# Two attention outputs and their values, copied and scaled in other places, in a hand-ordered pipeline

## The reference, cut to what matters

```
x = x + tanh(g0[0]) * attention_0(context, context, layernorm(x))   # A: 16 heads, softmax over the HEADS
x = x + tanh(g1[0]) * gated_mlp(layernorm(x))                       # B: silu(gate) * up, hidden width 768
x = x + tanh(g0[1]) * attention_1(layernorm(x), context)            # C: 16 query heads, one key and value head
x = x + tanh(g1[1]) * (layernorm(x) @ (W + low_rank).T + b)         # D
```

## Time and profile before

| | |
|---|---|
| median of 3 runs | 2359.47 us (2358.21 to 2359.94) |
| the profiled execution | 2358.72 us, of which the traced span is 2356.9 us |
| busy in the span | PE 98%, DVE 93%, POOL 75%, ACT 72% |
| granted TensorE clock | 0.999 of full speed over the span |
| start, loop of 57 iterations, end | about 165, 2009 and 183 us of the span |

### The profile page before, as it was taken

The page is one execution under the profiler, slowest core; times in us unless marked ns, Lnnn a source line. Parts: engine busy times, 40 slices in busy tenths (PEclk is TensorE's granted clock), DMA queues, the critical chain, the costliest instruction groups (busy, mean ns, idle before and its releaser), DMA issues.

```text
span 2356.9 us, 69621 instructions
## 1 busy us (share of the span) xinstructions
PE 2308.5 (98%) x27827; PEld 2062.3 (87%) x27827; DVE 2200.9 (93%) x3613; ACT 1705.6 (72%) x3402; POOL 1777.8 (75%) x2512
## 2 busy tenths in 40 slices
PE   6999999999999999999999999999999999999998
PEld 5888888889888888888889889889889889889887
DVE  6999999999999999999999999999999999999973
ACT  4667777777777777777777777777777777777664
POOL 3767787787787787787787777777778778778754
PEclk9999999999999999999999999999999999999999
DMA  3000010010010010010010100100100100000000
GB/s 110 28 22 28 29 34 27 29 34 27 29 34 27 29 34 27 29 34 27 31 33 27 34 29 27 34 29 27 34 29 28 33 29 30 31 29 32 20 22 15
DMA packets 74332, 73.33 MB, mean 31 GB/s; under 512 B 6555, under 2 KB 73393, under 8 KB 74290
## 3 DMA queue, kind: packets, MB, share of 16 engines
q1 hardware_dynamic: 74290, 72.75, 9.9%
HBM read 54.90 MB, written 16.78 MB: 30 GB/s over the span
## 4 chain that ended last, share of the span: by engine, by line
PE 56%; DVE 37%; issue 3%; ACT 1%; POOL 1%; DMA 1%; SPq 0%; POOLq 0%; DVEq 0%; ACTq 0%
DVE m L1600 11%; PE work L2383 10%; PE work L2384 9%; PE work L2385 9%; PE scores L2480 6%; PE work L2513 5%; PE work L2500 5%; DVE scores L1597 5%; DVE m L1591 4%; PE work L2420 4%; PE scores L2470 4%; DVE x L1628 4%; PE work L2398 2%; DVE stats_B L1559 2%; DVE stats_D L1559 2%
## 5 line engine op out<-in xcount | busy, mean ns | idle before, releaser
L856 ACT ACTIVATE e<-scores 120x1024 f32<-120x1024 f32 x512 | 517.5, 1042 | 35.9 <-DVE scores L1597 21.5
L2383 PE MATMUL work<-xt_hi_B,w_hi 128*128 128x256 f32 x1536 | 445.0, 290 | 2.8 <-POOL xt_lo_B L426 2.8
L2384 PE MATMUL work<-xt_lo_B,w_hi 128*128 128x256 f32 x1536 | 426.9, 278 | 0.0
L2385 PE MATMUL work<-xt_hi_B,w_lo 128*128 128x256 f32 x1536 | 426.6, 278 | 0.0
L413 POOL TENSOR_TENSOR zt<-e 120x512 f32<-120x512 f32 x256 | 331.1, 1295 | 49.5 <-ACT e L856 40.9
L407 POOL TENSOR_TENSOR h_lo<-h_f,h_hi 128x256 fp32r<-128x256 f32 x384 | 278.9, 740 | 90.5 <-ACT h_hi L803 90.4
L1597 DVE TENSOR_TENSOR scores<-scores,m 120x1024 f32<-120x1024 f32 x256 | 303.0, 1227 | 4.2
L2383 PEld LDWEIGHTS work<-xt_hi_B,w_hi 128*128 128x128 f32 x1536 | 290.8, 189 | 17.0 <-POOL xt_lo_B L426 13.5
L1609 DVE TENSOR_TENSOR e<-e,work 120x2048 f32<-120x2048 f32 x128 | 291.4, 2276 | 0.2
L1591 DVE TENSOR_REDUCE m<-scores 120x128 fp32r<-120x2048 f32 x128 | 290.0, 2266 | 0.9 <-PE scores L2470 0.8
L2384 PEld LDWEIGHTS work<-xt_lo_B,w_hi 128*128 128x128 f32 x1536 | 289.3, 188 | 0.0
(11 more groups left out here) (224 smaller groups left out, 7290.6 us busy)
## 6 DMA issues: line engine op xcount, KB each, us to landing
x_ln<-xp SPq DMA_DIRECT2D x64, 256.0 KB, 2.9
x_res<-xp SPq DMA_DIRECT2D x64, 256.0 KB, 2.8
y<-y_out SPq DMA_DIRECT2D x64, 256.0 KB, 2.2
ctx_f_A<-cp SPq DMA_DIRECT2D x64, 128.0 KB, 2.1
ctx_f_C<-cp SPq DMA_DIRECT2D x64, 128.0 KB, 2.0
qm<-mT SPq DMA_DIRECT2D x256, 4.0 KB
e<-wi SPq DMA_DIRECT2D x3, 768.0 KB, 7.1
w_ctx<-wc SPq DMA_DIRECT2D x1, 656.0 KB
```

Of the source, the lines that this page charges most:

```text
L856: return act.activation(e[0:SC, c, 2 * h:2 * h + 2, :, :].rearrange("p a b n -> p (a b n)"), scores[0:SC, 2 * h:2 * h + 2, :].rearrange("p ...
L2383: pe.matmul(out, a_hi, b_hi_, start=first, stop=False, skip_group_check=parts)
L2384: pe.matmul(out, a_hi, b_lo_, start=False, stop=False, skip_group_check=parts)
L2385: last = pe.matmul(out, a_lo, b_hi_, start=False, stop=end, skip_group_check=parts)
```

## The change

- `attended0`'s result is copied out of PSUM whole by ScalarE (`attended_out`, into `y0f`, which lies where the raw key weights of A lay in `w_ctx`); `y_hi["A"]` is then rounded from that copy, and `y_lo["A"]` is made by GpSimd (`attended_lo`), no longer by VectorE.
- C's values are made with A's: the two weights lie side by side in `w_ctx`, and `values0` has 272 columns in place of 256. `keys_values1` becomes `keys1`. Since A runs several rows ahead of C, the 16 columns pass through a ring of three small tiles (`v1_ring`), moved on by ScalarE once in each iteration, before they land in `v1_one`. `w_ctx` is loaded by four DMAs in place of one.
- The reciprocals of C's sums are written to PSUM (`W[1]`), and `weigh` reads them there; `rz_q` is gone.
- The order of all five streams is new, with other banks; the loop is cut at another place (it begins before `gate_up(4)`, no longer before D's product) and has 56 iterations.

```diff
-DEPTH = 7
+DEPTH = 8
-CSEG = {"k0": 0, "v0": KC * D, "k1": 2 * KC * D, "v1": 2 * KC * D + KC * P}
+CSEG = {"k0": 0, "v0": KC * D, "k1": KC * D + KC * (D + HD)}
+        v1_ring = sb("v1_ring", [P, 3, HD])
-        rz_q = sb("rz_q", [P, KC, 2, S // 32])
+        y0f = w_ctx[:, CSEG["k0"]:CSEG["k0"] + KC * D].rearrange("p (k n) -> p k n", k=KC)
...
-            sp.dma_start(w_ctx[:, :], wc).then_inc(s["ld_cst"], 16)
+            both_values = w_ctx[:, CSEG["v0"]:CSEG["k1"]].rearrange("p (k n) -> p k n", k=KC)
+            sp.dma_start(w_ctx[:, 0:KC * D], wc[:, FROM["k0"]:FROM["v0"]]).then_inc(s["ld_cst"], 16)
...
+            def attended_lo():
+                return pool.tensor_tensor(y_lo["A"][:, :, :], y0f[:, :, :], y_hi["A"][:, :, :].bitcast(F32), ALU.subtract)
...
+            def attended_out(bank):
+                return act.activation(y0f[:, :, :], two(bank, KC), ACT.Copy)
...
             def values1_out(bank):
-                return act.activation(v1_one[0:SC, 0:HD], bank[0:SC, P:P + HD], ACT.Copy)
+                return act.activation(v1_ring[0:SC, 0, :], bank[0:SC, D:D + HD], ACT.Copy)
+            def values1_on(i):
+                to = v1_ring[0:SC, i + 1, :] if i < 2 else v1_one[0:SC, 0:HD]
+                return act.activation(to, v1_ring[0:SC, i, :], ACT.Copy)
...
-            def reciprocal1():
-                return dve.reciprocal(rz_q[:, :, :, :], yz_q[:, :, :, :, HD])
+            def query_sums(bank):
+                return bank[:, 0:KC * 2 * (S // 32)].rearrange("p (c h q) -> p c h q", c=KC, h=2)
+            def reciprocal1(bank):
+                return dve.reciprocal(query_sums(bank), yz_q[:, :, :, :, HD])
...
             def values0(bank):
-                    last = pe.matmul(bank[:, 0:D], ctx_f["A"][:, kc, :], wc_of("v0", kc * D, D),
+                    last = pe.matmul(bank[:, 0:D + HD], ctx_f["A"][:, kc, :], wc_of("v0", kc * (D + HD), D + HD),
...
-                for kc in range(KC):
-                    last = pe.matmul(bank[:, P:P + HD], ctx_f["C"][:, kc, :], wc_of("v1", kc * HD, HD),
```

More of the change, by code:

```diff
@@ L1983, in _ @@
                 mean_variance("D").then_inc(s["ln_eps_D"], 1)
-                low(y_lo["A"][:, :, :], two(W[1], KC), y_hi["A"][:, :, :]).then_inc(s["yA_lo"], 1)
                 dve.wait_ge(s["M1_mm"], t)
@@ L2341, in _ @@
+            key_max(0).then_inc(s["M0_max"], 1)
             dve.wait_ge(s["woC_mm"], LAST + 6)
@@ new lines, in _ @@
+            pe.wait_ge(s["yz1"], 9)
+            gate_up(W[1], 5).then_inc(s["G_mm5"], 1)
+            pe.wait_ge(s["y_weighed"], 9)
+            pe.wait_ge(s["T_lo_C"], 9)
+            queries(W[3], "C", "q1").then_inc(s["q_mm_C"], 1)
+            pe.wait_ge(s["yA_out"], 9)
+            down(W[2], 0)
+            down(W[2], 1)
+            pe.wait_ge(s["yC_lo"], 9)
+            pe.wait_ge(s["ends_act"], 66)
+            rows_out(W[0], y_hi["C"], y_lo["C"], "wo1").then_inc(s["woC_mm"], 1)
+            down(W[2], 2)
@@ new lines, in _ @@
+            down(W[2], 3)
+            pe.wait_ge(s["A0_exp"], 20)
+            key_scores(1).then_inc(s["M1_mm"], 1)
+            down(W[2], 4)
+            pe.wait_ge(s["G_lo5"], 9)
+            down(W[2], 5).then_inc(s["dn_mm5"], 1)
+            rows_out(W[1], y_hi["A"], y_lo["A"], "wo0").then_inc(s["woA_mm"], 1)
+            values0(W[0]).then_inc(s["v0_mm"], 1)
+            pe.wait_ge(s["M1_max"], 9)
+            key_scores(0).then_inc(s["M0_mm"], 1)
+            pe.wait_ge(s["ln_D"], 9)
+            transposes(W[3], "D").then_inc(s["T_mm_D"], 1)
@@ new lines, in _ @@
+            pe.wait_ge(s["yA_out"], LAST + 3)
+            pe.wait_ge(s["ld_ctx_C"], 16 * (LAST + 3))
+            keys1(W[0]).then_inc(s["kv1_mm"], 1)
+            pe.wait_ge(s["yC_lo"], LAST + 3)
+            rows_out(W[3], y_hi["C"], y_lo["C"], "wo1").then_inc(s["woC_mm"], 1)
+            pe.wait_ge(s["ends_act"], 7 * LAST + 23)
+            down(W[2], 0)
+            down(W[2], 1)
+            down(W[2], 2)
+            down(W[2], 3)
+            pe.wait_ge(s["A0_exp"], 2 * LAST + 8)
+            key_scores(1).then_inc(s["M1_mm"], 1)
@@ new lines, in _ @@
+            down(W[2], 4)
+            pe.wait_ge(s["G_lo5"], LAST + 3)
+            down(W[2], 5).then_inc(s["dn_mm5"], 1)
+            pe.wait_ge(s["res_C"], LAST + 3)
+            rows_out(W[3], y_hi["A"], y_lo["A"], "wo0").then_inc(s["woA_mm"], 1)
+            pe.wait_ge(s["M1_max"], LAST + 3)
+            key_scores(0).then_inc(s["M0_mm"], 1)
+            pe.wait_ge(s["ln_D"], LAST + 3)
+            transposes(W[1], "D").then_inc(s["T_mm_D"], 1)
+            pe.wait_ge(s["res_B"], LAST + 3)
@@ new lines, in _ @@
+            pe.wait_ge(s["ld_ctx_C"], 16 * (LAST + 4))
+            keys1(W[0]).then_inc(s["kv1_mm"], 1)
+            pe.wait_ge(s["y_weighed"], LAST + 4)
+            down(W[2], 0)
+            down(W[2], 1)
+            pe.wait_ge(s["G_h4"], LAST + 4)
+            pe.wait_ge(s["T_lo_C"], LAST + 4)
+            queries(W[3], "C", "q1").then_inc(s["q_mm_C"], 1)
+            pe.wait_ge(s["ends_act"], 7 * LAST + 29)
+            pe.wait_ge(s["yC_lo"], LAST + 4)
+            rows_out(W[0], y_hi["C"], y_lo["C"], "wo1").then_inc(s["woC_mm"], 1)
@@ L3075, in _ @@
[L3075 to L3084 removed]
+            pe.wait_ge(s["ln_D"], LAST + 6)
```

3309 lines of the change are left out of this document (1803 added, 1506 removed), and 10 rows, old and new, of the table given.

## The result

The changed kernel takes 2332.23 us (median of 4 runs, 2331.37 to 2333.18), the kernel before in the same sessions 2358.84 us. The ratio is 0.9888, 95% interval 0.9874 to 0.9902: 1.1% faster, 0.8 us from the predicted 2333.0. The sum was nearly exact, but not every reason for it: the experiments show a third condition that the prediction did not have, and several of its smaller terms were wrong. So part of this closeness is luck.

What follows compares the result with a forecast made beforehand. VectorE and TensorE were taken to bound the loop in turn. -0.50 + 0.10 = -0.40 us per iteration, times 57 = -22.8, and -2.9 for the ends take the span from 2356.9 to 2331.2: 2333.0 us as an execution, range 2317 to 2348.

Steps and rivals of the forecast that it cites:

- VectorE's half, -0.50: From `yz_q` to `scores0(1)`: moving `y_lo["A"]` to GpSimd saves 0.50 us per iteration, limited by `key_scores(1)`.
- TensorE's account, -0.30: TensorE, per iteration: C's value matmuls save 0.37 us, wider `values0` costs 0.07; VectorE still releases `scores0(1)` last by 0.1.
- the rival in which TensorE becomes the bound: Loop: the iteration is what TensorE needs, 34.62 us, in all 2321 us; chance 0.15.
- `T_lo_B` late by 0.10: TensorE's half: `x_biased` ahead of `xt_lo_B` on GpSimd makes `T_lo_B` late, +0.10 us per iteration.
- Its upper bound: `T_lo_B`'s delay on GpSimd: at most 0.67 us per iteration, if only the last gap holds; half the gain gone.
- the range of this case: Whole kernel, the prediction's own case, chance 0.58: 2323 to 2344 us, from the bounds of `T_lo_B` and the ends.
- ScalarE's chain, nothing: ScalarE's new copy and moved keys cost nothing; `y_lo["C"]` is ready about 0.1 us before TensorE wants it.
- Reciprocals in PSUM, nothing: VectorE's reciprocals of C's sums, written to and read from PSUM, cost no more than in SBUF.
- A fixed price of 65 ns for PSUM: Rival on VectorE's half: reciprocal and two `y_q` cost 65 ns more each, +11 us, 2344 us; chance 0.05.
- The collision with `attended_lo`: Rival on VectorE's half: GpSimd's `attended_lo` holds up `y_q`, +0.54 us per iteration, 2364 us; chance 0.05.
- The ends, -2.9: Start and end: -2.1 us from TensorE's savings, +1.5 for SyncE's DMA issues, -2.3 for fewer fillers; together -2.9.
- the prediction's own signs of being wrong: Profile signs listed beforehand, among them a start over 165.5 us by more than 2, or its granted clock under 0.98.

Runs made afterwards that it cites:

- run 3: Kernel before, C's value matmuls and VectorE's `y_lo["A"]` both left out of the loop: ratio 0.9970, iteration 35.18 us.
- run 4: Kernel before with both those removals, and GpSimd's sum `y_out + x_biased` moved ahead of `y_lo["C"]`: ratio 0.9885, iteration mean 34.80 us.
- run 7: Changed kernel with four more matmuls on TensorE ahead of the wait for `M0_max`: ratio 0.9966 to the kernel before, iteration 35.22 us.
- run 6: Kernel before with four more matmuls on TensorE ahead of the wait for `M0_max` in the loop: ratio 1.0056, iteration 35.55 us.
- run 8: Changed kernel with the reciprocals of C's sums back in SBUF: ratio 0.9988 to the kernel before, iteration mean 35.22 us.
- run 11: Changed kernel with the four loads of `w_ctx` issued behind the fourth round of weights: ratio 0.9898 to the kernel before.
- run 12: Changed kernel with 22 filling matmuls in a gap of TensorE's start: ratio 0.9906 to the kernel before.
- run 9: Changed kernel with `y_lo["A"]` back on VectorE, from the copy in SBUF: ratio 0.9990 to the kernel before, iteration mean 35.30 us.

## Why the prediction was right, and where it was not

*VectorE's half, -0.50:* right in size and place: 0.48 measured, limited by `key_scores(1)` as it said, with 0.21 us of wait where its own sum left 0.08. But that VectorE's and TensorE's halves are all there is was wrong for the kernel before, as runs 3 and 4 show.

*TensorE's account, -0.30:* it was 0.39 or 0.40, since C's keys with values took 0.91 us start to start and the keys alone take 0.46 (1018.36 to 1018.82), with `values0` at 1.02 for 0.96. That VectorE still releases `scores0(1)` last, by about 0.1, holds: 0.06 by run 7. The wait before it was taken at 0.31 from the weight load's row; run 6 gives 0.13. The two errors offset each other (0.13 + 0.39 - 0.48 = 0.04 us left, by its own figures 0.31 + 0.30 - 0.50 = 0.11). So the rival in which TensorE becomes the bound was nearer in kind than its 2321 us, and its price too high: what it could have saved beyond the forecast was the wait that is left, 0.06 x 56 = 3.4 us, not 0.2 us per iteration.

*`T_lo_B` late by 0.10:* wrong. `xt_lo_B` starts 1037.21 - 1033.90 = 3.31 us behind `scores0(1)`, before 3.30, each time right behind ScalarE's `xt_hi_B`. That half did lose 0.08 us, elsewhere: `scores1(0)` now stands behind the second gate product, not the third, and from the first gate product of the row to the second `scores1` group it takes 8.84 us in place of 8.77, start to start, with one change of operand more. That this change is the cause is read from the trace and not tried. The term of 0.10 stands for nothing that happened, and the 0.08 that was lost elsewhere fits it by luck. Its upper bound was also misread: with 0.67 not half of the gain is gone but all of it, 0.67 - 0.50 = 0.17 us per iteration slower. And the range of this case does not add up: 11 and 3 us above 2333 are 2347, not 2344.

*ScalarE's chain, nothing:* right. `y_lo["C"]` ends 0.21 us ahead of its first product; there is no wait for it in the loop.

```profile
1021.60 1.30 POOL L624 TENSOR_TENSOR y_lo_C<-y1f,y_hi_C 128x512 fp32r<-128x512 f32 x1 [0.69 <-ACT y_hi_C L883]
```

*Reciprocals in PSUM, nothing:* right as a price. The first argument for it was empty, though: a line laid through 957 ns for 128 numbers and 354 ns for 32 leaves the same rest at both, whatever PSUM costs. What shows the price is the run. By form, after:

```profile
L1864 DVE TENSOR_TENSOR y_q<-yz_q,work 128x256 f32<-128x256 f32 x128 | 48.1, 417 | 2.1
L1860 DVE RECIPROCAL work<-yz_q 128x32 f32<-128x32 f32 x64 | 23.2, 362 | 2.1
```

417 ns and 362 ns stand against 419 and 354 before. The two rivals built on it are out. A fixed price of 65 ns for PSUM, which the table in "VectorE: DVE Perf Modes" of the Trainium skill, section on the TRN2 errata, would give (an estimate from its 120 and 58 cycles at 0.96 GHz), does not show: -2 and +8 ns. The collision with `attended_lo` comes only where both inputs lie in SBUF (run 8), and there it costs 0.39 us per iteration over 34.83 and not the rival's 0.54, since `key_max(1)` waits anyway.

*The ends, -2.9:* -3.7 by the traces (-26.5 in all, less 22.8), from parts of which at least two were wrong. The issues of SyncE cost nothing by the trace: TensorE's product from the last weights starts at 22.25 us, before at 22.65 (run 11 could not show it, for it delayed `w_ctx`). And the start, with 25 fillers fewer, is no shorter. There one of the prediction's own signs of being wrong came true: the granted clock over the start is 0.95, under its 0.98, and by `xt_lo_D` the start is more than 2 us longer. In the changed kernel TensorE is busy for 2.3 of the 8 us from 44 to 52 us, and its granted clock falls to 0.50, which is 1.2 GHz, from 48 to 60 us; in the kernel before it is busy for 7.4 of these 8 and the clock stays at 1.00. Windows of 2 us, the number behind DVE, ACT and POOL is PEclk:

```profile
46.00:48.00 2.00, 0.75 (x28) 0.56 (x21) 1.18 (x1) 1.37 (x5) 1.92 (x5) 0.79 0.00 0
48.00:50.00 2.00, 0.63 (x3) 0.63 (x4) 1.97 (x2) 1.32 (x3) 1.92 (x3) 0.50 0.00 0
...
58.00:60.00 2.00, 2.00 (x35) 1.76 (x32) 2.00 (x1) 0.00 (x0) 1.09 (x4) 0.50 0.00 0
```

A's queries there take 3 us at 0.21 us a matmul, and 1.5 in run 12, where the clock was back at 1.00. How much of the longer start is the clock's stays open, since run 12's fillers cost more than they gave. The start ended 2.2 us later, the drain of the last seven rows 5.6 us sooner: its distances of `xt_lo_D` sum to 208.4 us, before 213.9. Seven rows at the loop's 0.40 would be 2.8 of these; the rest I did not take apart. That the ends came within 1 us of the forecast is luck.

*What the prediction lacked* is the step from "two chains alternate" to "nothing else is near". It took the slack of TensorE and ScalarE to a tenth and never wrote down GpSimd's. With the old order the same removals give 0.05 us per iteration (run 3), with the new one 0.40. The forecast was worked out on the new order, and that order happens to keep GpSimd's chain out of the way; nothing in the working shows that it would. That was luck.

## What to carry to other kernels

Where all engines are over 70% busy and one pattern repeats, list for every wait of the pattern how much earlier the producer is done; a gain can only be as large as the smallest of these margins outside the part that you shorten. Here a margin of 0.1 to 0.2 us on an engine that was 75% busy left 0.05 us of a gain of 0.4 (run 3). Price a moved instruction at the place it leaves as well as at the one it enters, and do not read a wait of the weight load as lost time of the matmuls: fill it and see.

## What was not expected of the hardware

A collision costs both sides: in run 9 the VectorE operation from SBUF lasted 0.88 us against the 0.66 of the one from PSUM, and GpSimd's `zt` beside it 1.73 against 1.28.

In runs 11 and 12 the loop did not run at 34.83 us from its start: 14 of the first iterations in run 11 and 4 in run 12 took 35.03, and then it fell to 34.83 with no instruction changed. TensorE was busy throughout in both stretches and its granted clock 1.00; in run 11 some groups of twelve matmuls took 0.04 to 0.05 us longer in the slower one (1.50, 1.42 and 1.41 us, in the other 1.45, 1.37 and 1.36), and two groups took 0.04 and 0.06 less. That may be why the times scatter from 2333.9 to 2342.3 us in run 11 and from 2334.6 to 2342.5 in run 12. What selects between the two was not found, and stays open.
